# A graph layer with an expert layer behind it: the old maxima of the edge walk become a fifth entry in PSUM, and three smaller edits in the later stages

## The reference

```python
# layer 1: attention over edges, 8 heads of 32
x = x + gnn(layernorm(x))
    logits = einsum('ehd,ehd->eh', q[dst], k[src]) / sqrt(32)
    seg_max = segment_max(logits, dst);  expv = exp(logits - seg_max[dst])
    agg = segment_sum(expv / segment_sum(expv, dst)[dst] * v[src], dst)
    h = gelu(agg + x @ Wskip + bskip);   y = layernorm(x + h) * gamma + beta
# layer 2: scores from a small graph attention, then the two best of four experts
x = x + ffn(layernorm(x))
    e = leaky_relu(a_src[src] + a_dst[dst]);  softmax over dst;  scores = layernorm(sums + b_gat)
    out = sum over 4 experts of gate * (gelu(x @ W1 + b1) @ W2 + b2)
```

## Time and profile before

| what | us |
|---|---|
| time of the kernel, median of 3 runs (3986.79 to 3992.12) | 3990.57 |
| the profiled execution, its own time | 3987.74 |
| its span, first to last instruction | 3985.9 |
| PE busy | 3324.8 (83%) |
| DVE busy | 3352.4 (84%) |
| ACT busy | 2563.2 (64%) |
| POOL busy | 2589.5 (65%) |

### The profile page before, as it was taken

One profiled execution on the slowest core, in us unless ns is written; L12 is line 12 of the kernel. 1 busy time (PEld: TensorE's weight loads), 2 busy tenths in 40 slices (PEclk: granted clock), 3 DMA queues, 4 the chain that ended last, 5 costly groups with the idle time before them and its releaser, 6 DMA issues. The chain is left out here.

```text
span 3985.9 us, 106539 instructions
## 1 busy us (share of the span) xinstructions
PE 3324.8 (83%) x26108; PEld 2449.2 (61%) x26109; DVE 3352.4 (84%) x8812; ACT 2563.2 (64%) x6745; POOL 2589.5 (65%) x2730
## 2 busy tenths in 40 slices
PE   7886999999999999999999992488888888887620
PEld 2334888888788888878888872455555555554410
DVE  8886999999999999999999998667766667666448
ACT  5435888888788888878888875455555555554310
POOL 3225777777677777777777742277777777777750
PEclk9898999999999999999999995599999999999855
DMA  6536888888888888888888857211111111111148
GB/s 218 191 130 200 255 260 256 259 256 261 242 257 255 262 257 257 253 246 257 257 258 258 259 175 246 70 23 33 32 33 32 29 33 33 33 28 33 23 94 309
DMA packets 367692, 683.52 MB, mean 171 GB/s; under 512 B 70294, under 2 KB 240482, under 8 KB 367074
## 3 DMA queue, kind: packets, MB, share of 16 engines
q0 software_dynamic: 157888, 427.05, 38.9%
q1 hardware_dynamic: 183106, 223.68, 16.6%
q10 hardware_dynamic: 26080, 25.70, 2.2%
HBM read 588.41 MB, written 87.78 MB: 170 GB/s over the span
## 5 line engine op out<-in xcount | busy, mean ns | idle before, releaser
L746 POOL DMA_INDIRECT KV<-kv_d,src_i x1564 | 1478.9, 946 | 536.0 <-issue 472.9
L1396 POOL DMA_INDIRECT re_src<-src_tab_d,rsrc x1024 | 982.4, 959 | 312.0 <-issue 244.3
L1012 PE MATMUL agg_ps<-msg,oh 128*128 128x264 f32 x3512 | 889.9, 396 | 1.7 <-DVE agg_ps L830 1.7
L1012 PEld LDWEIGHTS agg_ps<-msg,oh 128*128 128x128 f32 x3512 | 631.6, 190 | 87.5 <-ACT oh L921 1.9
L965 PE MATMUL Q<-q,ohT 128*128 128x256 bf16 x5328 | 659.0, 274 | 1.7
L907 ACT ACTIVATE square<-iota_b,off 128x128 bf16<-128x128 bf16 x1784 | 569.3, 392 | 0.3
L847 DVE TENSOR_REDUCE lg<-prod 128x32 f32<-128x1024 f32 x443 | 540.5, 1220 | 15.3
L835 DVE TENSOR_TENSOR msg<-KV,weigh_ps 128x1056 f32<-128x1056 f32 x439 | 542.5, 1236 | 8.0 <-issue 7.8
L843 DVE TENSOR_TENSOR prod<-KV,Q 128x1024 f32<-128x1024 f32 x443 | 532.6, 1202 | 17.6 <-POOLq L737 13.2
L965 PEld LDWEIGHTS Q<-q,ohT 128*128 128x128 bf16 x5328 | 492.1, 98 | 61.0 <-issue 0.5
L1618 PE MATMUL ex_y_ps<-ex_w,ex_hid 128*112 128x256 f32 x1792 | 440.7, 389 | 0.0
(11 more groups left out here) (264 smaller groups left out, 5662.8 us busy)
## 6 DMA issues: line engine op xcount, KB each, us to landing
q<-q_d SPq DMA_DIRECT2D x446, 192.0 KB
y_d<-ex_y ACTq DMA_DIRECT2D x56, 448.0 KB
KV<-kv_d,src_i POOLq DMA_INDIRECT x1564
nu_xs<-xs_d SPq DMA_DIRECT2D x7, 2688.0 KB, 11.6
rg_ye<-y_d SPq DMA_DIRECT2D x5, 3584.0 KB, 15.6
re_src<-src_tab_d,rsrc POOLq DMA_INDIRECT x1024
kv_d<-pr_kv SPq DMA_DIRECT2D x49, 260.0 KB, 2.2
xs_d<-pr_xs SPq DMA_DIRECT2D x49, 256.0 KB, 2.3
```

The source lines that it names most:

```text
L746: pool.indirect_dma_start(out=KV[:, t % (KVR * G), :], out_offset=None, in_=k.kv_d, in_offset=bass.IndirectOffsetOnAxis(ap=k.src_i[:, t:t ...
L1012: m = pe.matmul(agg_ps[:, 0:HEADS * HW], oh32[ring(s, 2)][:, t, :], msg[ring(s, 2)][:, t, :, :].rearrange("p h e -> p (h e)"), start=False ...
L1396: pool.indirect_dma_start(out=gs[:, t % (RING * RG), :], out_offset=None, in_=k.src_tab_d, in_offset=bass.IndirectOffsetOnAxis(ap=k.rsrc[: ...
```

## The change

It has four parts.

1. The edge walk. `m_all`, the table of the maxima of all nodes, goes. `m_old` (two buffers) holds the maxima that step `s` starts from; ACT makes it from the last step's `m_new` plus `fresh`, which is 0 within a window and a very large number where the walk enters a new one. `max_ps` gets a fifth group of 8 columns behind the four tiles' (`old_ps`), into which PE copies `m_old` by a product with the identity (`old_maxima`). DVE's one reduction over five entries (`new_maxima`) gives `m_new`; `raise_max` and DVE's `fall` are gone. PE makes the fall in PSUM from `m_new` and `m_old` by products with the identity and its negative (`fall`), and ACT's `factor` reads it there. Signs in `maxima` are turned so that all five entries are negated maxima. The semaphore `maxima` is now raised by `old_maxima`.
2. node_update. The first block's `xs` rows are loaded ahead of the constants and in three pieces; its division (`quotients`) stands ahead of DVE's wait for the constants; the second norm, the transposes, the copies and the products go by parts of 4 and 3 windows.
3. route_experts. The maximum over the partitions is made by a PE transpose, a DVE reduction, a diagonal and a PE product with ones; `partition_all_reduce` goes, and POOL's gathers wait for nothing of it.
4. route_gates. The three rows of constants are loaded at the start of route_experts. The last window of each block of 7 is summed by PE (five f32 products with diagonals of the gates that ACT makes) and copied out by ACT, so DVE has 24 instructions a block; ACT issues the stores.

```diff
 # attend, DVE
-                def tile_maxima(s):
+                def new_maxima(s):
                     v.wait_ge(ok["maxima"], s.v + 1)
-                    v.tensor_reduce(tile_max[:, :], max_ps.rearrange("p (t h) -> p h t", h=HEADS), AX.X, ALU.max).then_inc(ok["tile_max"], 1)
-                def raise_max(s):
...
-                def fall(s):
...
+                    v.tensor_reduce(m_new[ring(s, 2)][:, :], max_ps.rearrange("p (t h) -> p h t", h=HEADS), AX.X, ALU.min).then_inc(ok["m_new"], 1)
                 def body(s, last):
                     if there(s):
-                        tile_maxima(s)
+                        new_maxima(s)
                     if there(s + 1):
                         segment_max(s + 1)
                     if there(s + 2):
                         scan(s + 2)
-                    if there(s):
-                        raise_max(s)
                     if there(s + (-1)):
                         message(s + (-1))
                         scale_sums(s + (-1))
-                    if there(s):
-                        fall(s)
                     product(s + 4)
                     logits(s + 4)
 # attend, ACT
-                def keep_max(s):
...
+                def reference(s):
+                    act.wait_ge(ok["m_new"], s.v)
+                    act.activation(m_old[ring(s, 2)][:, :], m_new[ring(s + (-1), 2)][:, :], ACT.Identity, bias=fresh[:, bass.ds(s.v, 1)]).then_inc(ok["m_old"], 1)
+                def factor(s):
+                    act.wait_ge(ok["fall"], s.v + 1)
+                    act.activation(fac[ring(s, 2)][:, :], fall_ps, ACT.Exp, scale=SCALE).then_inc(ok["fac"], 1)
 # attend, PE
+                def fall(s):
+                    if there(s + (-1)):
+                        pe.wait_ge(ok["fac"], s.v)
+                    pe.matmul(fall_ps, k.ident_b[:, :], m_new[ring(s, 2)][:, :], start=True, stop=False)
+                    pe.matmul(fall_ps, minus_b[:, :], m_old[ring(s, 2)][:, :], start=False, stop=True).then_inc(ok["fall"], 1)
+                def old_maxima(s):
+                    if there(s + (-1)):
+                        pe.wait_ge(ok["m_old"], s.v)
+                    pe.matmul(old_ps, k.ident_b[:, :], m_old[ring(s, 2)][:, :], start=True, stop=True).then_inc(ok["maxima"], 1)
                 def maxima(s):
...
-                        m = pe.matmul(at, hot, seg_max[ring(s, 2)][:, t, :], start=False, stop=(t == G - 1))
-                    m.then_inc(ok["maxima"], 1)
+                        pe.matmul(at, hot, seg_max[ring(s, 2)][:, t, :], start=False, stop=(t == G - 1))
                     if there(s):
                         differences(s)
+                        fall(s)
                     if there(s + (-1)):
                         sums(s + (-1))
                     turn(s + 7)
+                    if there(s + 1):
+                        old_maxima(s + 1)
 # node_update, SP and DVE
+                for at, sem in ((D, skip_in), (0, landed[0]), (2 * D, landed[0])):
+                    sp.dma_start(xs[0][:, :, at:at + D], k.xs_d[0:CN, at:at + D].rearrange("(w p) f -> p w f", p=P)).then_inc(sem, 16)
                 sp.dma_start(gam[:, :], bc(gamma.unsqueeze(0), [P, D])).then_inc(const, 16)
...
-                load(0, 0)
+                quotients(0, 0)
+                v.wait_ge(const, 80)
 # node_update, ACT (PE's transposes and products likewise)
-                    normalise(1, x2[s], xn2).then_inc(xn_ok, 1)
+                    for a, b in parts:
+                        normalise(1, x2[s], xn2, a, b).then_inc(xn_ok, 1)
 # route_experts, POOL and PE
-                pool.wait_ge(ok["max_in"], 1)
-                pool.partition_all_reduce(peak[:, 1, :], peak[:, 0, :], P, bass.bass_isa.ReduceOp.max).then_inc(ok["max"], 1)
+                pe.wait_ge(ok["max_in"], 1)
+                pe.transpose(d_ps[0][0:RH, 0:P], peak[:, :], k.ident[:, :]).then_inc(ok["max"], 1)
+                pe.wait_ge(ok["max_in"], 2)
+                pe.matmul(d_ps[1][:, 0:RH], ones[:, :], peak_diag[:, :], start=True, stop=True).then_inc(ok["max"], 1)
 # route_gates, DVE, PE and ACT
-                v.wait_ge(landed, 48)
+                v.wait_ge(k.first_in, 80)
-                        for w in range(CW):
+                        for w in range(VT):        # VT = CW - 1
+                    pe.matmul(sum_ps[i % 2][:, 0:D], k.ident[:, :], o[s][:, VT, :], start=True, stop=False)
+                    for e in range(NE):
+                        m = pe.matmul(sum_ps[i % 2][:, 0:D], diag[i % 2][:, e, :], ye[s][:, VT, e, :], start=False, stop=(e == NE - 1))
+                    act.copy(o[i % SLOTS][:, VT, :], sum_ps[i % 2][:, 0:D]).then_inc(a_ok, 1)
```

More of the change, by code:

```diff
@@ L869, in body @@
                         group(s + 5)
[L871 to L875, removed]
+                v.memset(msg[1][:, 0, :, :], 0.0).then_inc(ok["zeroed"], 1)
+                v.memset(m_old[0][:, :], 2.0 * BIG).then_inc(ok["zeroed"], 1)
+                v.tensor_scalar(minus_b[:, :], k.ident_b[:, :], -1.0, None, ALU.mult).then_inc(ok["zeroed"], 1)
+                v.memset(fresh[:, STEPS:NS], 0.0)
+                v.tensor_tensor(fresh[:, 1:STEPS], k.wbase[:, 1:STEPS], k.wbase[:, 0:STEPS - 1], ALU.not_equal).then_inc(ok["zeroed"], 1)
+                v.wait_ge(ok["zeroed"], 5)
+                v.tensor_scalar(fresh[:, 1:STEPS], fresh[:, 1:STEPS], 2.0 * BIG, None, ALU.mult).then_inc(ok["zeroed"], 1)
+                walk(v, body, 4, groups.clear)
+                groups.clear()
                 message(LAST)
@@ L932, in body @@
                     if there(s):
-                        act.wait_ge(ok["m_fall"], s.v + 1)
-                        act.activation(fac[ring(s, 2)][:, :], m_fall[ring(s, 2)][:, :], ACT.Exp, scale=SCALE).then_inc(ok["fac"], 1)
-                        keep_max(s)
+                        reference(s + 1)
+                        factor(s)
                     if there(s + 6):
@@ L1190, in turn @@
                     v.wait_ge(s_gelu, i + 1)
+                    if first and s == 0:
+                        v.wait_ge(landed[0], FIRST_ROWS)
                     ch.on(v.tensor_tensor(out[s][:, :, :], out[s][:, :, :], xs[s][:, :, 0:D], ALU.add))
@@ L1240, in turn @@
                     act.wait_ge(back, i * KB + SHIFT)
-                    normalise(0, out[s], x2[s]).then_inc(norm, 1)
+                    normalise(0, out[s], x2[s], 0, CW).then_inc(norm, 1)
                     if not (first and s == 0):
@@ L1651, in _, with route_gates @@
                 walk(pe, body)
-def route_gates(nc, k, b_gat, ln_gamma, ln_beta, out):
+def route_gates(nc, k, out):
     with ExitStack() as ctx:
@@ L1708, in _, with factors, store @@
                 step(3, u4[:, :, :], t4[:, :, :], ACT.Exp)
+                def factors(i):
+                    for e in range(NE):
+                        f = act.activation(diag[i % 2][:, e, :], k.ident[:, :], ACT.Copy, scale=k.gates[:, i * CW + VT, e:e + 1])
+                    f.then_inc(a_ok, 1)
+                def store(i):
+                    s = i % SLOTS
+                    act.wait_ge(added, (i + 1) * NE * VT)
+                    act.wait_ge(a_ok, copied(i))
+                    if i + 1 < NB:
+                        act.dma_start(out[i * CN:(i + 1) * CN, :].rearrange("(w p) f -> p w f", p=P), o[s]).then_inc(stored[s], 16)
+                    else:
+                        act.dma_start(out[i * CN:(NW - 1) * P, :].rearrange("(w p) f -> p w f", p=P), o[s][:, 0:CW - 1, :]).then_inc(stored[s], 16)
+                        act.dma_start(out[(NW - 1) * P:N, :], o[s][0:TAIL, CW - 1, :]).then_inc(stored[s], 16)
+                act.wait_ge(a_in, 4)
+                factors(0)
+                factors(1)
+                for i in range(NB):
+                    act.wait_ge(summed, i + 1)
+                    act.copy(o[i % SLOTS][:, VT, :], sum_ps[i % 2][:, 0:D]).then_inc(a_ok, 1)
+                    if i + 2 < NB:
+                        factors(i + 2)
+                    store(i)
+            @block.tensor
+            def _(pe):
+                for i in range(NB):
+                    s = i % SLOTS
+                    arrived(pe, i)
+                    pe.wait_ge(a_ok, diag_made(i))
+                    if i >= 2:
+                        pe.wait_ge(a_ok, copied(i - 2))
+                    pe.matmul(sum_ps[i % 2][:, 0:D], k.ident[:, :], o[s][:, VT, :], start=True, stop=False)
+                    for e in range(NE):
+                        m = pe.matmul(sum_ps[i % 2][:, 0:D], diag[i % 2][:, e, :], ye[s][:, VT, e, :], start=False, stop=(e == NE - 1))
+                    m.then_inc(summed, 1)
             @block.vector
@@ L1810, in graph_layers @@
         with ExitStack() as walk:
-            k.negbig = sb(walk, "negbig", [P, TG], BF16)
+            k.far = sb(walk, "far", [P, TG], BF16)
             k.ones_b = sb(walk, "ones_b", [P, P], BF16)
@@ L1820, in graph_layers @@
             k.last_tab = sb(walk, "last_tab", [1, NG], I32)
```

(3 more changed lines are left out.)

168 lines of the change are left out of this document (84 added, 84 removed).

## The result

The changed kernel takes **4350.4 us** (median of 5 runs, 4348.9 to 4351.6) against 3990.6 before: a ratio of 1.0902, 95% interval 1.0887 to 1.0917. It is slower, by 360 us, and lies in the predicted range; the point was 30 us too low. The profiled execution has a span of 4347.0 us.

A forecast was written before the change was run, and what follows sets the result against it. DVE was taken as the bound, PE close behind. From 3987.7 us: walk +351, ACT +1, node_update -4, route_experts -6, route_gates -12 gives 4318; with 2.8 from profiled run to median, 4320 us, range 4265 to 4435 (80%).

The forecast's parts named there:

- The ring: Edge walk: PE's body end, new maxima, segment maximum, scan, PE's next head form one closed ring, 5.33 us a step.
- PE's body with the added products: Edge walk, term of the ring: PE's body 4.49 us, the added products 0.06.
- the hand-over from PE to DVE: Edge walk, term of the ring: from PE's last product to DVE's new maxima, 0.04 us.
- DVE's share: Edge walk, term of the ring: new maxima to segment maximum 0.10 us, to the scan 0.09, the scan 0.40.
- The stalls: Edge walk: stalls were left as they are, with no added time.
- ACT's 1: Head of the edge walk: ACT waits for six small preparations, 1 us more.
- the lower of the two sums: route_gates: if store and load take as long as now, the gain is 9.2 us; otherwise 18.8; 12 was taken.
- the chain through store and load: route_gates: the last block's load waits for the third block's store to land; if unchanged, the gain is 9.2 us.
- DVE's relief: Edge walk, rival: the ring does not close and DVE's shorter list counts, 35 us less, 3934 in all; chance 6%.
- TensorE's clock: Edge walk, rival: granted clock falls to a mean of 0.93, 127 us more over the walk, 4447; chance 8%.
- ACT's `factor`: Edge walk, sign against the prediction: others wait for `factor`, which waits for PE's `fall`; by up to 0.75 us without the ring.

The follow-up runs named there:

- e1: Changed kernel with PE's product that fills the fifth entry moved ahead of the four transposes of the one-hots: 4250.7 us.
- e5: Changed kernel with the product that fills the fifth entry made five times in place, behind the transposes: 4386.3 us.
- e7: Changed kernel with one more DVE instruction between the new maxima and the segment maximum: 4392.1 us.
- e6: e2 with the product that fills the fifth entry made five times in place of one: 3954.8 us.
- e8: Changed kernel with the same added DVE instruction as e7, but at the end of DVE's body, behind the logits: 4350.8 us.
- e2: Changed kernel with the fifth-entry product behind the fall, ahead of the sums, and ACT's old maxima made ahead of the sums' copy: 3951.1 us.
- e4: Changed kernel with the edge walk and its preparations as before the change, the three later stages as changed: 3973.1 us.
- e9: e2 run again unchanged, as the base for later runs: 3953.4 us.
- e3: Changed kernel with only PE's half of e2: product behind the fall, ACT's old maxima left late: 4296.5 us.
- e10: e2 without PE's and ACT's share of the gated sum in route_gates, so DVE has 28 instructions a block: 3957.4 us.

## Why the prediction was right, and where 30 us went

**The ring** was right in kind: e1, e5 and e7 change the time by about what they take out of the ring or put into it, e6 and e8 put the same work outside of it and change nothing that can be told, and e2 opens it. Its links are means from the starts and ends of L952, L976 and L799, over the 425 of 439 steps that no stall lengthened (those under 5.6 us):

| link | predicted | measured |
|---|---|---|
| PE's body with the added products, L952 to the end of L976 | 4.49 + 0.06 | 4.554 |
| PE to DVE, end of L976 to L799 | 0.04 | 0.066 |
| L799 to the next L952 | 0.10 + 0.09 + 0.40 + 0.15 | 0.777 |
| step | 5.33 | 5.397 |

The body was sized rightly. The two mis-sized terms are the hand-over from PE to DVE, read off a single row, and DVE's share: behind the reduction of 40 columns the segment maximum starts after 0.117 and not 0.10, the scan after another 0.107 and not 0.09, while the scan and its hand-over to PE take 0.55, as read. Together that is 0.07 a step. The stalls, which I left as they are, did stay: they add 0.06 to the mean step in both kernels (4.593 against 4.53 before, 5.458 against 5.397 now). So the mean step grew by 0.865 and not by 0.80, and the walk by 379 us (341.1 to 2390.2, now 338.5 to 2766.8) and not by 352 (351 and ACT's 1): this is 27 of the 30 us.

**The later stages.** node_update is 0.4 us shorter (167.2 to 166.8), not 4. At its head DVE's sum with `xs` starts 13.4 us after the stage's first instruction (2780.46 against 2767.1), before 13.0 (2403.53 against 2390.5): the rows are issued 2.3 us earlier in the stage and cost no wait, but now DVE waits for the constants behind them, 9.55 us. At its end the products follow the transposes without the wait of before, but the products took 6.14 us and not 4.25: the granted clock from 2926 to 2934 was 0.50, and from 2552 to 2558 before it was 0.74. route_experts is 7.0 shorter (predicted 6; 3 to 8 in the eleven other kernels). route_gates is 8.4 shorter (predicted 12, and 9.2 by the lower of the two sums): I should have stayed with the chain through store and load. With prepare 2.6 us shorter by chance (336 to 342 over all profiles) and 1.6 instead of 2.8 us between profile and median, these make the 30.

**The rivals.** Where the ring is open DVE's relief seems to count: e2 is 22 us below e4 and e9 20, though I gave it 35; no run takes this relief alone. TensorE's clock did not fall: its granted share over the walk is 0.99, and 1.00 from 400 to 1150 us, with PE idle 0.84 us in each step of 5.4. The Trainium skill, page "TensorE: Matmul & The Clock Gate", section "HAM oscillation — how this bites in real kernels", warns of repeated idle gaps; gaps of this length did no harm here. That ACT's `factor` would hold others up did not come true, but e3 shows that ACT's list was near: it closes a ring as soon as PE asks for the old maxima where ACT makes them late.

What stays open is what sets e2's step, which mostly lies between 4.39 and 4.7 us: DVE's list (4.39), POOL's gathers (4.45) and PE's body (4.35 to 4.45) lie too near each other to be told apart by these runs. That the loads set the pace of route_gates is read from DVE's waits in e9 and e10; no run changes the loads alone.

## What to carry to other kernels

When a signal is moved, find the last instruction that raises it and the first that waits for it, and follow the lists around until you are back: if the way closes within one step, its length is the step, and no engine's busy share will show it. Work in such a ring costs its time however idle its engine is, and work outside costs nothing while its engine has idle time left; so before an instruction is made cheaper, ask where it stands. Here one product, moved up a list with the copy that feeds it, was worth 400 us and turned the change into a gain of 0.9%. Moved without that copy it was worth 54 us only (e3), since a second ring nearly as long stood behind the first.

## What the runs showed of the hardware

Four small products more behind their like cost 0.083 us a step, 0.02 each (e5), though PE's timeline spaces the four over 0.104: DVE's reduction started 0.037 us behind the printed end of the last product and not 0.066 as behind a single one. The same DVE instruction took 0.18 us at the head of the body (e7) and 0.36 at its end (e8). And at the end of node_update TensorE stood at the lower of its two levels for all of the 28 products (granted 0.50), 0.21 us apart; before, 19 of them ran at the full clock, 0.11 us apart, and the 28 took 1.9 us less.
